# A fused attention and expert kernel: transposing the softmax shift one step behind its maxima, and moving low halves and weight splits

## What is computed

```python
n = layernorm(x)
q, k1, v1 = n @ Wq1, n @ Wk1, n @ Wv1          # 128 -> 512 = 8 heads x 64
k2, v2 = ctx @ Wk2, ctx @ Wv2
k, v = concat([k1, k2]), concat([v1, v2])      # 768 keys
attn = softmax(q . k / 8)                      # per head
x = x + tanh(g_xattn) * ((attn @ v) @ Wo + bo)
n = layernorm(x)
top_w, top_i = top_k(n @ gate_w + gate_b, 2)   # softmax of the two weights -> combine
out = sum_e combine[:, e] * (gelu(n @ w1[e] + b1[e]) @ w2[e] + b2[e])
x = x + tanh(g_ffn) * (out + gelu(n @ ws1 + bs1) @ ws2 + bs2)
```

## Time and profile before

| | us |
|---|---|
| runs shown, median (lowest to highest) | 178.49 (177.58 to 178.78) |
| the profiled execution, its own time | 177.47 |
| its span, first to last instruction | 175.6 |

### The profile page before, as it was taken

The page is one execution under the profiler, slowest core; times in us unless marked ns, Lnnn a source line. Parts: engine busy times, 40 slices in busy tenths (PEclk is TensorE's granted clock), DMA queues, the critical chain, the costliest instruction groups (busy, mean ns, idle before and its releaser), DMA issues.

```text
span 175.6 us, 4599 instructions
## 1 busy us (share of the span) xinstructions
PE 143.3 (82%) x1911; PEld 108.4 (62%) x1911; DVE 116.7 (66%) x222; ACT 114.5 (65%) x183; POOL 123.6 (70%) x97
## 2 busy tenths in 40 slices
PE   7759783988998979598797984999939949999953
PEld 4513342336755456476585773898738939999942
DVE  1776796477686867737486185999986526554792
ACT  2464888497896877658688885977553435556510
POOL 5489666849699888766856967554497397778760
PEclk9996999699999999969999999999965999999999
DMA  5599906100004000000000000000000000100001
GB/s 148 169 348 315 293 7 185 53 0 4 4 11 114 4 0 4 0 4 0 4 0 4 4 0 0 4 0 4 0 0 6 2 0 4 30 4 0 4 0 30
DMA packets 10238, 7.73 MB, mean 44 GB/s; under 512 B 1085, under 2 KB 8426, under 8 KB 10218
## 3 DMA queue, kind: packets, MB, share of 16 engines
q1 hardware_dynamic: 10218, 7.44, 14.2%
HBM read 7.18 MB, written 0.26 MB: 42 GB/s over the span
## 4 chain that ended last, share of the span: by engine, by line
PE 49%; DVE 19%; ACT 13%; POOL 7%; issue 5%; DMA 3%; SPq 2%; DVEq 0%; ACTq 0%
PE banks L950 9%; PE banks L952 9%; PE banks L951 9%; DVE part L787 5%; ACT prob L624 4%; DMA ring<-in_L_xattn_Wq_dram 3%; PE banks L1120 3%; PE banks L1074 3%; DVE k_both L771 3%; ACT p_hi L632 3%; POOL k_both L564 2%; PE banks L1122 2%; PE banks L1121 2%; PE banks L1080 2%; PE banks L1077 2%
## 5 line engine op out<-in xcount | busy, mean ns | idle before, releaser
L516 POOL TENSOR_TENSOR p_lo<-prob,p_hi 128x1024 f16<-128x1024 f32 x23 | 48.9, 2130 | 18.6 <-ACT p_hi L632 18.6
L564 POOL TENSOR_TENSOR k_both<-prob,k_both 128x1024 f16<-128x1024 f32 (+1 forms) x18 | 38.4, 2138 | 11.4 <-DVE k_both L898 11.4
L688 ACT ACTIVATE prob<-banks,b1T 128x256 f32<-128x256 f32 x72 | 28.4, 476 | 17.4 <-PE banks L952 15.3
L787 DVE TENSOR_REDUCE part<-banks 128x2 f32<-128x1024 f32 (+1 forms) x24 | 29.3, 1219 | 7.0 <-PE banks L1044 5.1
L950 PE MATMUL banks<-wf,k_both 128*128 128x128 f16 x144 | 26.3, 225 | 7.6 <-POOL k_both L564 6.3
L624 ACT ACTIVATE prob<-banks 128x1024 f32<-128x1024 f32 x24 | 24.6, 1024 | 8.9 <-PE banks L1088 8.7
L898 DVE CAST k_both<-prob 128x1024 f16<-128x1024 f32 (+1 forms) x19 | 17.2, 909 | 14.4 <-ACT prob L688 14.2
L951 PE MATMUL banks<-wf,k_both 128*128 128x128 f16 x144 | 26.2, 225 | 0.0
L952 PE MATMUL banks<-wf,k_both 128*128 128x128 f16 x144 | 26.2, 224 | 0.0
L632 ACT ACTIVATE p_hi<-prob 128x1024 f16<-128x1024 f32 x24 | 25.4, 1057 | 0.8
L1120 PE MATMUL banks<-v_hi,p_hi 128*128 128x65 f16 x192 | 19.9, 198 | 1.2 <-DVE o_sb L815 1.2
(11 more groups left out here) (151 smaller groups left out, 332.9 us busy)
## 6 DMA issues: line engine op xcount, KB each, us to landing
ring<-in_L_ffn_w_dram SPq DMA_DIRECT2D x16, 256.0 KB, 4.1
wf<-in_ctx_dram SPq DMA_DIRECT2D x2, 256.0 KB, 5.4
ring<-in_L_xattn_Wk_dram SPq DMA_DIRECT2D x2, 256.0 KB, 4.3
ring<-in_L_xattn_Wv_dram SPq DMA_DIRECT2D x2, 256.0 KB, 6.3
ring<-in_L_ffn_ws_dram SPq DMA_DIRECT2D x2, 256.0 KB, 6.2
x_sb<-in_x_dram SPq DMA_DIRECT2D x1, 256.0 KB, 3.0
ring<-in_L_xattn_Wq_dram SPq DMA_DIRECT2D x1, 256.0 KB, 5.6
ring<-in_L_xattn_Wo_dram SPq DMA_DIRECT2D x1, 256.0 KB, 7.1
```

Of the source, the lines that this page charges most:

```text
L516: nc.gpsimd.tensor_tensor(p_lo[:, u % RINGP, :, :].rearrange("p a n -> p (a n)"), prob[:, u % RINGE, :], p_hi[:, u % RINGP, :, :].rearrang ...
L564: nc.gpsimd.tensor_tensor(hid_lo[:, k % HB, cols], hid[:, k % 2, cols], hid_hi[:, k % HB, cols], ALU.subtract).then_inc(hl_done, 1)
L688: nc.scalar.activation(hid[:, k % 2, c * T1:(c + 1) * T1], span(2 * (k % 2), HC * T1)[:, c * T1:(c + 1) * T1], ACT.Gelu, bias=b1T[:, e * H ...
L787: nc.vector.tensor_reduce(dst, src, AX_X, ALU.max).then_inc(part_done, 1)
```

## The change

The walk begins one step earlier (CHUNK0 = -4), so all chunks come a step earlier relative to the scores, while the shift row stays where it was: one step behind chunk 2. The shift row is transposed into the last 128 columns of bank 6, beside the values, and no longer into bank 0; chunk 0 now waits for the last reduction alone. On PE the order in a step is scores, values, shift row, chunk, projections, warm matmuls. On DVE the low halves of a step's projections are made at the head of the next step, then tail, shift, reciprocals and normalise, and the reduction last. The table of projections is rearranged over steps and banks (v items now use banks 4, 5 and 7, none bank 6). The DMA of Wq is issued ahead of the gates and bo; ACT splits Wq before the tanh of the gates; the splits of Wv2 and Wv1 move to step -1 and that of Wo behind step 1 (POOL's part to step 2); POOL makes the first expert's low half before that of Wv2. Warm matmuls: 4 new ones ahead of the first chunk, and 2, 4, 8, 0 in place of 2, 4, 5 in the negative steps.

```diff
-CHUNK0 = -UPP
+CHUNK0 = -(UPP + 1)
...
 LATE = {
-    -3: [(("k", 0, 1), 4)],
-    -2: [(("q", 1), 7)],
-    -1: [(("v", 0, 0), 6)],
-    0: [(("v", 0, 1), 6), (("v", 0, 2), 7)],
-    1: [(("k", 0, 2), 4)],
-    2: [(("q", 2), 7), (("v", 0, 3), 6)],
-    3: [(("v", 0, 4), 6), (("v", 0, 5), 7)],
-    4: [(("k", 0, 3), 4)],
-    5: [(("q", 3), 7), (("tc", 1), 4)],
+    -4: [(("k", 0, 1), 4)],
+    -3: [(("q", 1), 7)],
+    0: [(("k", 0, 2), 4), (("q", 2), 7)],
+    1: [(("v", 0, 0), 4), (("v", 0, 1), 5), (("v", 0, 2), 7)],
+    2: [(("v", 0, 3), 4), (("v", 0, 4), 5)],
+    3: [(("v", 0, 5), 7)],
+    4: [(("k", 0, 3), 4), (("q", 3), 7)],
+    5: [(("tc", 1), 7)],
     6: [(("k", 1, 0), 4)],
-    7: [(("v", 1, 0), 7), (("v", 1, 1), 4)],
+    7: [(("v", 1, 0), 4), (("v", 1, 1), 5), (("v", 1, 2), 7)],
     8: [(("k", 1, 1), 4)],
-    9: [(("v", 1, 2), 7), (("v", 1, 3), 4)],
-    10: [(("k", 1, 2), 4)],
-    11: [(("v", 1, 4), 7), (("v", 1, 5), 4)],
-    12: [(("k", 1, 3), 4)],
+    9: [(("v", 1, 3), 7)],
+    10: [(("v", 1, 4), 4), (("v", 1, 5), 5)],
+    11: [(("k", 1, 2), 4)],
+    13: [(("k", 1, 3), 4)],
 }
...
-WARM_START, WARM_LAYERNORM, WARM_STEP = 14, 9, (2, 4, 5)
+WARM_START, WARM_LAYERNORM, WARM_MAX, WARM_STEP = 14, 9, 4, (2, 4, 8, 0)
...
     if s >= 0:
-        return late_items(s)
+        return late_items(s - 1)
...
+SPLIT_BY_ACT = {1: [WK2, WK1]}
...
+        shift_ps_rows = banks[:, 6, 512 - P:]
...
-            for w in (WK2, WK1):
+            for w in (WK2, WK1, WQ):
                 load_a(w)
...
-            for w in (WQ, WV2):
-                load_a(w)
+            load_a(WV2)
...
+            early_lo(0)
             lo_by_pool(WV2)
-            early_lo(0)
             lo_by_pool(WV1)
...
-                if i == 1:
+                if i == 2:
                     lo_by_pool(WO)
...
             for n in range(len(PRE)):
-                if n == 2:
+                item_of(n)
+                if n == 1:
+                    split_a(WQ)
                     tanh_gates()
-                item_of(n)
-            scaled_for_pool(WV2)
...
                 if i == -1:
+                    scaled_for_pool(WV2)
                     scaled_for_pool(WV1)
-                    scaled_for_pool(WO)
                 for n in late_items(i):
                     item_of(n)
+                if i == 1:
+                    scaled_for_pool(WO)
...
-                    in0=banks[:, 0, 0:P].unsqueeze(1).broadcast_to([P, QT, P]), scalar=SHIFT_P * SHIFT_ROW,
+                    in0=shift_ps_rows.unsqueeze(1).broadcast_to([P, QT, P]), scalar=SHIFT_P * SHIFT_ROW,
...
+                if i >= 0:
+                    for n in items_at(i):
+                        item_of(n)
+                for b, s in tail_of(i - 1):
+                    tail(b, s)
+                for b, s in tail_of(i):
+                    tail_first(b, s)
+                if shift_of(i) is not None:
+                    shift_out(shift_of(i))
+                if values_of(i) is not None:
+                    reciprocals(values_of(i))
+                    normalise(values_of(i))
                 if chunk_of(i) is not None:
                     p, c = chunk_of(i)
                     part_max(p, c)
                     if c == UPP - 1:
                         whole_max(p)
-                if shift_of(i) is not None:
-                    shift_out(shift_of(i))
-                for b, s in tail_of(i - 1):
-                    tail(b, s)
-                for b, s in tail_of(i):
-                    tail_first(b, s)
-                if values_of(i) is not None:
-                    reciprocals(values_of(i))
-                    normalise(values_of(i))
-                for n in items_at(i):
-                    item_of(n)
+                if i < 0:
+                    for n in items_at(i):
+                        item_of(n)
...
+            keep_warm(WARM_MAX, 2)
...
-                    if p == 0:
-                        read_out(before(NI, [0, 1]))
-                    else:
-                        pe.wait_ge(shift_done, p)
+                if p == 0 and c == 0:
+                    read_out(before(NI, [0, 1]))
                 else:
                     pe.wait_ge(part_done, UPP * p + c)
...
-                nc.tensor.transpose(banks[:, 0, 0:P], nmax[:, p % 2, :], ident[:, :]).then_inc(shift_ps, 1)
+                if p == 0:
+                    read_out(before(NI, [6]))
+                nc.tensor.transpose(shift_ps_rows, nmax[:, p % 2, :], ident[:, :]).then_inc(shift_ps, 1)
...
             for i in range(CHUNK0, STEPS):
-                if i % UPP == UPP - 1 and chunk_of(i) is not None:
-                    max_chunk(*chunk_of(i))
                 if 0 <= i < NU:
                     scores(i)
-                if i % UPP != UPP - 1 and chunk_of(i) is not None:
-                    max_chunk(*chunk_of(i))
...
                     if k == 0:
-                        pe.wait_ge(shift_done, NPAIR)
+                        pe.wait_ge(part_done, UPP * NPAIR)
...
-                if i < 0:
-                    for n in late_items(i):
-                        item_of(n)
-                    keep_warm(WARM_STEP[i - CHUNK0], 2)
                 if shift_of(i) is not None:
                     shift_row(shift_of(i))
-                if i >= 0:
-                    for n in late_items(i):
-                        item_of(n)
+                if chunk_of(i) is not None:
+                    max_chunk(*chunk_of(i))
+                for n in late_items(i):
+                    item_of(n)
+                if i < 0:
+                    keep_warm(WARM_STEP[i - CHUNK0], 2)
```

More of the change, by code:

```diff
@@ L591, in item_of @@
                 item = ITEMS[n]
-                for w in SPLIT_BEFORE.get(n, []):
+                for w in SPLIT_BY_ACT.get(n, []):
                     split_a(w)
```

## The result

| | before | changed |
|---|---|---|
| median, us (lowest to highest) | 178.04 (177.42 to 178.78) | 165.81 (165.6 to 166.18) |
| profiled execution: span, us | 175.6 | 164.1 |
| mean granted clock | 0.951 | 0.979 |

The ratio is 0.9314, 95% interval 0.9268 to 0.936: 12.2 us or 6.9% faster. (Ratios here leave out the more disturbed runs of a kernel; where one differs from the ratio of the medians, the text goes by medians and profiles.) I had forecast 171.0 with a range from 167: the direction and the mechanism are right, the size is outside the range, too small.

The account below looks back on a forecast made before the run. Bound: a ring of scores, exp, high half, DVE and PE, with PE's issue order deciding who waits. Gain 9.4 - 1.4 - 0.5 = 7.5 us from 177.47 gives 170.0, plus 1.0 for the median: 171.0, range 167 to 175.5.

Parts of the forecast that it names:

- replay: Start and attention: new order laid out by hand with profiled durations at full clock; FFN begins at 93.0, gain 9.4 us.
- the step on the transpose: Attention: transposing the maxima a step behind their last chunk should remove PE's 5.3 us of waits on nmax.
- The replay has none ... I put one back, at 1.4 us: Ahead of the FFN: allowance for one remaining stretch of slow PE clock, taking 1.4 us off the gain.
- 24 steps of imperfect handoffs: Attention: allowance of 0.02 us a step for handoffs between engines, taking 0.5 us off the gain.
- The change touches nothing behind it: FFN, 73.20 us: code behind attention is untouched, so the gain can come only from attention, the start and slow clock.
- The clock decides: Rival, 168 us, chance 0.13: less idle PE keeps full clock in start and attention; the FFN's slow stretch halves too.
- The slower rival: DVE in attention: reduction last in its order delays PE's next chunk, 0.6 us at 20 steps; 181 us, chance 0.04.
- only the nmax wait goes: Rival in attention: 5.3 us go, 1.3 return as waits on ACT, the start gains only 0.5; 174 us, chance 0.11.
- Bank 6, 0 us: Attention: values and shift row sharing this bank add no new wait; 0 to 3 us possible, 0 taken.
- Low halves a step later, ahead of the reduction: DVE in attention: they find ACT's results nearly ready, but PE waits on reductions some 3 us in all, at worst 12.
- Wq first, 0.5: Start: issuing Wq's DMA earlier brings the q projection and first chunk 0.5 us earlier; 0 to 1.4 possible.
- The tanh, "cost 0": Start, on ACT: the gates' tanh goes 0.7 us later, with POOL's work behind it, at no cost.

Follow-up runs that it names:

- the experiment without the lead: The changed kernel with chunks of maxima starting at step -3 again and DVE's reduction ahead of tail and shift: 180.1 us, ratio 1.0399 to the kernel before.
- the filled kernels: The kernel before with dummy matmuls in PE's idle places: three places ahead of the FFN, 173.6 us; these and three in the FFN, 171.07 us.
- the same kernels filled: Dummy matmuls in the FFN's three long gaps of the changed kernel, 164.85 us; in these and three earlier gaps of the kernel before, 171.07 us.
- the filled kernel before: The kernel before with dummy matmuls in six idle places of PE, three ahead of the FFN and three in it: 171.07 us.
- the job with all four kernels: On one chip: kernel before 176.83 us, the same with six gaps filled with dummies 171.07, changed kernel 166.25, the same with the FFN's gaps filled 164.55.
- the other order: The changed kernel with the reduction ahead of tail, shift and normalise on DVE, still behind the low halves: 172.59 us.
- the two filled kernels before: The kernel before with dummy matmuls in three idle places of PE, 173.6 us, and in six, three of them in the FFN, 171.07 us.

## Why the prediction was right, and where it was wrong

The span shrank by 11.5 us; I forecast 7.5 = 9.4 (replay) - 1.4 (one slow stretch put back) - 0.5 (handoffs).

The median came 5.2 us under the 171.0. No single term explains that: with the largest of them put right, 169.6 would have been forecast.

- *The replay, 9.4 us.* It came to 10.5, with every boundary in the table within 1.1 us. The wait on nmax went, as the step on the transpose had it, and the experiment without the lead shows that the rest doesn't hold without it. The replay is long by about 0.05 us a step.
- *"The replay has none ... I put one back, at 1.4 us."* This is the step that failed. None came back in attention of the changed kernel (clock 1.00 in its window), nor in the profiles of the four further runs with the same order. I put a stretch back for gaps of "over 1 us at a time", though two of the three stretches of before had stood behind gaps of 1.8 and 2.4 us. The price, up to 1.7 for each, was right (1.5 to 1.6). Moreover I didn't say that the replay, at full clock, already held three of them as gain: by the filled kernels 3.9 to 4.8 of its 10.5 us are the clock.
- *"24 steps of imperfect handoffs": 0.5.* The profile shows nothing of it. The durations between rows have the handoffs in them; I took them twice.
- *"The change touches nothing behind it"*: the FFN's code is the same, but it lasts 1.0 us less (72.20 against 73.20) with 6.8 us of slow clock in either (one stretch of 6.8 before, two of 3.4 now). Against the same kernels filled (71.15 and 71.37 us) they cost 1.05 now and 1.8 before: where they fall matters. The sum 1.1 + 1.4 + 0.5 + 1.0 is the 4.0 between 7.5 and 11.5. The last 0.7 up to 12.2 is in the medians: the profiled execution of before, 177.47, was 0.6 under its median of 178.04. I had put the median of the changed kernel 1.0 above its profiled execution too; it is 0.1 below.
- *"The clock decides" (168, chance 0.13).* The Trainium skill (TensorE: Matmul & The Clock Gate, What's actually happening) says that activity releases the throttle. The trace agrees: clock 1.00 over 73.10 us in which PE's waits are at most 1.0 us, and the filled kernel before at 1.0. I took it for an extra beside the order; it is 4.1 of the 10.6 us in the job with all four kernels, and 5.7 of the 12.2 if the order was worth the same there. Against this rival I had said that "the start has the same gaps still"; no profile of the same order has a stretch there.
- *The slower rival, and "only the nmax wait goes",* fell: waits on reductions are 2.1 us, and the reduction last on DVE is worth 5.0 us ahead of the FFN, a slow stretch of the other order included. PE's new wait on ACT is 1.4 us, 1.1 of it from Wo's splits, as in the replay.
- *Bank 6, 0 us:* right, no wait on it is among those of the changed kernel; without it 3.8 us are lost.
- *"Low halves a step later, ahead of the reduction", some 3 us of waits:* the waits are 2.1. But the reading was wrong: low halves were directly ahead of the next step's reduction before, too. What moved is the reduction, behind shift and values.
- *Wq first, 0.5:* the first chunk came 0.67 us earlier (12.40 for 13.07), but that doesn't confirm it: the two filled kernels before, with the old order, had it at 12.37 and 13.44. The start's 1.35 us can't be parted into order, clock and landings. *The tanh, "cost 0"*, costs up to 0.9: I moved its instructions in the sum but not its wait on the gates, whose DMAs go out 0.48 us later and whose landing then held k's high half.
- *Warm matmuls, 0:* right.

## What to carry to other kernels

Lay out the new order by hand with durations of the trace; it was right to 1.1 us over 24 steps. Then ask of each slow stretch of the TensorE clock which gap it followed and whether the gap is still there, in place of a flat allowance; where a small chain of another engine (a reduction, a transpose) ends in TensorE's queue, give it a whole step of lead and a bank that the work behind it doesn't write. A DMA that moves up the queue moves others down: follow who waits for those.

## What the runs showed of the hardware that I had not expected

- The kernel before took between 171.81 and 178.78 us, and its time follows the mean granted clock roughly: in one job 172.03 at 0.980, 173.99 to 174.14 at 0.970, 175.34 to 177.98 at 0.961, 175.82 to 177.92 at 0.951 to 0.952, 177.54 and 177.91 at 0.942. With the gaps filled it took 170.79 to 171.71. The same gaps slow the clock in one run and not in the next (a gap of 2.41 us near 99 us had a slow stretch behind it in one profile of the changed kernel and none in the other); filled, the time is steady to 1 us.
- In attention of the kernel before slow stretches of some 3.4 us at 1.2 GHz stood behind gaps of 1.8 and 2.4 us, and with dummies of 0.11 us in these gaps and at the start there was none, at a gain of 3.9 to 4.8 us ahead of the FFN. Whether the four at the start did anything is not shown: the kernel before with Wq first had no stretch there without them.
- A stretch cost 1.5 to 1.6 us in attention. In the FFN two together cost 1.05 us in one profile of the changed kernel and a single one elsewhere 1.5 in another, so the mean clock of a run doesn't give its time.
- The second gate, half a KB, issued at 3.72 behind five transfers of 256 KB, landed after 6.9 us (6.2 to 6.8 in three more profiles); issued at 3.25 behind four it took 5.5. Wq's 256 KB, issued just ahead of the two gates, took 4.7. Being small did not bring it in sooner; that the large ones ahead were the cause is not shown.
